# A two-layer mixture of experts around attention on one core: layer 0's first expert product gives its hidden values with inner channels in partitions, and both layers' gathers are issued one scatter earlier

## The reference, cut to what matters

```python
x = x + _L0_conv_ref(_gn(x), ...)          # layer 0: 1024 tokens of 192 channels
t = _to_tokens(x)
t = t + _L1_attn_ref(_ln_t(t), ...)        # 12 heads of 16
t = t + _L1_ffn_ref(_ln_t(t), ...)         # layer 1

def _L0_conv_ref(x, gate_w, fc1_w, fc1_b, fc2_w, fc2_b, ...):
    xf = x.reshape(-1, C)
    scores = softmax(xf @ gate_w.T)
    top_v, top_i = top_k(scores, 2)        # weights normalised to sum 1
    for e in range(8):
        w_e = sum(where(top_i == e, top_v, 0.0))
        h = _gelu(xf @ fc1_w[e].T + fc1_b[e])     # 192 -> 512
        y = h @ fc2_w[e].T + fc2_b[e]             # 512 -> 192
        out = out + w_e[:, None] * y
    shared = _gelu(xf @ w1_w.T + w1_b) * (xf @ w3_w.T + w3_b) @ w2_w.T + w2_b
    return out + shared
# layer 1: 16 experts, silu(x @ wg_e) * (x @ wu_e) @ wd_e with 384 inner channels, top 2, and a shared expert
```

## Time and profile before

| what | value |
|---|---|
| runs (3) | 442.01, 443.23, 445.12 us; median 443.23 |
| the profiled execution | 443.67 us, of which the span from first to last instruction 441.6 us |
| PE busy | 405.3 us (92%), granted clock 0.996 of full on average |
| DVE busy | 261.9 us (59%) |
| ACT busy | 186.4 us (42%) |
| POOL busy | 128.2 us (29%) |
| chain that ended last | PE 81%, ACT 6%, DVE 5%, DMA 5%, issue 2% |
| layer 0's blocks | first product of block 0 at 55.82 us, second product of block 22 at 143.25 us |

### The profile page before, as it was taken

How to read it: one execution, slowest core, us unless ns; L and a number is a source line. 1 busy time by engine, 2 the same in 40 slices (tenths; PEclk the granted TensorE clock), 3 DMA queues, 4 the chain that set the end, 5 groups by cost and what they waited for, 6 DMA issues and landing times.

```text
span 441.6 us, 7990 instructions
## 1 busy us (share of the span) xinstructions
PE 405.3 (92%) x2303; PEld 299.3 (68%) x2304; DVE 261.9 (59%) x673; ACT 186.4 (42%) x463; POOL 128.2 (29%) x137
## 2 busy tenths in 40 slices
PE   0899998999999999988888877999899999999996
PEld 0755455776776998866666655745677888878885
DVE  3526424222222286789898974474587777777743
ACT  1124231222222125898787863331444445454410
POOL 4300224555554100000000000001265555555540
PEclk9999999999999999999999999899999999999999
DMA  8999301111100496000000086870011111110006
GB/s 207 279 272 356 73 22 37 39 46 46 42 24 10 143 299 265 1 1 1 1 1 1 2 230 199 204 212 14 16 36 37 43 35 39 45 50 23 0 0 214
DMA packets 17432, 39.41 MB, mean 89 GB/s; under 512 B 5711, under 2 KB 10869, under 8 KB 16962
## 3 DMA queue, kind: packets, MB, share of 16 engines
q1 hardware_dynamic: 9186, 29.66, 22.8%
q0 software_dynamic: 5280, 6.85, 5.3%
q10 hardware_dynamic: 2944, 2.62, 1.8%
HBM read 36.21 MB, written 7.93 MB: 100 GB/s over the span
## 4 chain that ended last, share of the span: by engine, by line
PE 81%; ACT 6%; DVE 5%; DMA 5%; issue 2%; ACTq 0%; DVEq 0%; SPq 0%; POOLq 0%
PE bank L1376 13%; PE bank L1287 12%; PE bank L1349 9%; PE bank L1354 9%; PE bank L1549 5%; PE bank L1365 5%; PE bank L1503 4%; PE bank L1565 3%; PE bank L1331 3%; DMA w_first<-y_rows 3%; PE bank L1360 2%; PE bank L1359 2%; PE bank L1273 2%; PE bank L1597 2%; ACT xn_t L760 2%
## 5 line engine op out<-in xcount | busy, mean ns | idle before, releaser
L554 POOL DMA_INDIRECT rows<-xn_rows,slot_tok x56 | 59.7, 1066 | 89.4 <-DVE slot_tok L940 53.2
L562 POOL DMA_INDIRECT y_rows<-y,slot_row x54 | 55.4, 1027 | 79.1 <-DVE y L1008 41.9
L1376 PE MATMUL bank<-w_second,hid_t 128*128 x370 | 69.4, 327 | 2.8 <-DVE hid_t L993 2.8
L1376 PEld LDWEIGHTS bank<-w_second,hid_t 128*128 128x128 f32 x370 | 58.8, 190 | 3.6 <-issue 3.5
L1354 PE MATMUL bank<-w_first,rows_t 128*128 x124 | 45.3, 488 | 0.4 <-issue 0.4
L1010 DVE TENSOR_TENSOR y<-bank,w_second 128x192 f32<-128x192 f32 x23 | 8.2, 357 | 60.3 <-PE bank L1376 60.3
L993 DVE COPY hid_t<-bank 128x384 f32<-128x384 f32 (+1 forms) x54 | 33.0, 612 | 18.0 <-PE bank L1365 12.9
L1349 PE MATMUL bank<-w_first,rows_t 96*128 (+1 forms) x92 | 43.4, 594 | 0.1
L659 ACT ACTIVATE act_h<-bank 128x512 f32<-128x512 f32 x23 | 13.7, 597 | 65.0 <-PE bank L1349 65.0
L602 POOL COPY act_h<-o_inv 128x256 f32<-128x256 f32 x12 | 4.8, 400 | 121.7 <-DVE o_inv L1174 121.7
L664 ACT ACTIVATE act_g<-bank 128x384 f32<-128x384 f32 x31 | 15.2, 491 | 49.0 <-PE bank L1360 49.0
(11 more groups left out here) (198 smaller groups left out, 791.1 us busy)
## 6 DMA issues: line engine op xcount, KB each, us to landing
w_first<-in_gate_up SPq DMA_DIRECT2D x16, 384.0 KB, 5.8
w_second<-in_down SPq DMA_DIRECT2D x1, 4608.0 KB, 17.4
w_first<-in_fc SPq DMA_DIRECT2D x1, 3072.0 KB
w_second<-in_fc SPq DMA_DIRECT2D x1, 3072.0 KB, 29.0
w_first<-in_gate_up_rest SPq DMA_DIRECT2D x16, 192.0 KB, 6.5
rows<-xn_rows,slot_tok POOLq DMA_INDIRECT x56, 2.7
y_rows<-y,slot_row POOLq DMA_INDIRECT x54, 2.3
w_first<-in_x_t SPq DMA_DIRECT2D x2, 384.0 KB, 4.6
```

What stands on the lines that cost most here:

```text
L554: pool.indirect_dma_start(rows[b % 2][:, 0:ROW[L.l]], None, xn_rows[L.l], bass.IndirectOffsetOnAxis(slot_tok[:, b:b + 1].bitcast(U32), 0), ...
L562: pool.indirect_dma_start(y_rows[L.l], bass.IndirectOffsetOnAxis(slot_row[:, b:b + 1].bitcast(U32), 0), y[b % 2][:], None, bounds_check=TO ...
L1376: ins = pe.matmul(bank[:, 1, 0:C], hid_t[:, tile(ic)], w(P, ic * C, C), start=(ic == 0), stop=(ic == L.IC - 1))
```

## The change

In layer 0 the first product is turned round: the expert's 128 x 128 pieces of weights are held and the rows stream past, which gives the hidden values with inner channels in partitions. It takes 8 matmuls of 128 columns for the 2 of 512. Gelu writes them straight into the tile that the second product holds (`act_h` and `hid_t` in turn, `hid_b`); the 4 hidden transposes and DVE's copy go. A held operand is read here from a fixed place, so DVE copies the block's weights (97 x 1024 values, 2 instructions) from `w_first` into one of two buffers `first_w` two blocks ahead (`copy_weights`). The copies for blocks 0 and 1 come in front of the last shared product on DVE. In both layers POOL issues the gather of b+4 in front of the scatter of b.

```diff
+        hid_b = [act_h, hid_t]
+        first_w = [scratch_at(2048 + u * NCH * I0, NCH, I0) for u in range(2)]
...
             for b in range(L.NB):
-                scatter(b)
                 if b + AHEAD <= L.NB:
                     pool.wait_ge(L.rows_t_ps, b + AHEAD - 1)
                     gather(b + AHEAD)
+                scatter(b)
...
+        def act_block0(act, L, b, u):
+            act.wait_ge(L.first_ps, b + 1)
+            nc.scalar.activation(hid_b[u][:], bank[:, 5, :], ACT.Gelu).then_inc(L.hid_ready, 1)
...
+            def copy_weights(L, b, u):
+                at = dve.value_load(blk_weights[0:1, 0, bass.ds(b, 1)], min_val=0, max_val=(L.E - 1) * L.sizes[0])
+                if not isinstance(b, int) or b >= 2:
+                    dve.wait_ge(L.first_ps, b - 1)
+                for k in range(NCH):
+                    w = w_first[0:CH + k, k * I0:(L.E - 1) * L.sizes[0] + (k + 1) * I0][:, bass.ds(at, I0)]
+                    v.tensor_copy(first_w[u][0:CH + k, k, :], w).then_inc(L.first_w_ready, 1)
             def blocks(L):
                 dve.wait_ge(s_fc2b, 16)
-                dve.wait_ge(L.expert_ready, len(L.sizes))
-                hid_copy(L, 0)
+                copy_weights(L, 2, 0)
                 result(L, 0, 0, 0)
-                hid_copy(L, 1)
+                copy_weights(L, 3, 1)
                 result(L, 1, 1, 0)
                 w_low_parts()
-                with dve.Fori(0, (L.NB - 3) // 2) as i:
+                with dve.Fori(0, (L.NB - 5) // 2) as i:
                     for u in range(2):
-                        b = i * 2 + (u + 3)
-                        hid_copy(L, b - 1)
-                        result(L, b - 1, u, i + 1)
+                        b = i * 2 + (u + 4)
+                        copy_weights(L, b, u)
+                        result(L, b - 2, u, i + 1)
...
+                elif s == "first weights":
+                    dve.wait_ge(s_fc1, 32)
+                    dve.wait_ge(L.expert_ready, len(L.sizes))
+                    copy_weights(L, 0, 0)
+                    copy_weights(L, 1, 1)
...
                 pe.wait_ge(L.rows_t_ready, b + 1)
                 if L.l == 0:
-                    for k in range(NCH):
-                        kr = CH + k
-                        ins = pe.matmul(bank[:, 5, :], rows_t[0:kr, k, :], w(kr, k * I0, I0),
-                                        start=(k == 0), stop=(k == NCH - 1))
+                    pe.wait_ge(L.first_w_ready, NCH * (b + 1))
+                    if not isinstance(b, int) or b > 0:
+                        pe.wait_ge(L.hid_ready, b)
+                    for ic in range(L.IC):
+                        for k in range(NCH):
+                            kr = CH + k
+                            ins = pe.matmul(bank[:, 5, tile(ic)], first_w[u][0:kr, k, tile(ic)], rows_t[0:kr, k, :],
+                                            start=(k == 0), stop=(k == NCH - 1))
...
-            def second(L, b, w, first_block=False):
-                pe.wait_ge(L.hid_t_ready, b + 1)
+            def second(L, b, w, u, first_block=False):
+                hid = hid_t if L.l else hid_b[u]
+                pe.wait_ge(L.hid_t_ready if L.l else L.hid_ready, b + 1)
...
+            def blocks_first(L, down):
+                first(L, 0, None, 0)
+                rows_transpose(L, 1, 1, 0)
+                first(L, 1, None, 1)
+                rows_transpose(L, 2, 0, 1)
+                second(L, 0, down, 0, True)
+                down = weights(L, 1, 1)
+                first(L, 2, None, 0)
+                rows_transpose(L, 3, 1, 1)
+                second(L, 1, down, 1)
+                with pe.Fori(0, (L.NB - 3) // 2) as i:
+                    down = weights(L, i * 2 + 2, 1)
+                    for u in range(2):
+                        b = i * 2 + (u + 3)
+                        first(L, b, None, 1 - u)
+                        rows_transpose(L, b + 1, u, i + 2)
+                        second(L, b - 1, down, u)
+                        if u == 0:
+                            down = weights(L, b, 1)
+                second(L, L.NB - 1, weights(L, L.NB - 1, 1), (L.NB - 1) % 2)
```

More of the change, by code:

```diff
@@ L443, in build @@
                 ["best0", "best1", "top2", 0, "pads", 1, "ended", "expert", "blocks", "places", 2, "slots", 3, "weights", 4, "diag0", 5,
-                 "diag1", 6, 7]),
+                 "diag1", 6, "first weights", 7]),
             1: ([(0, 1), (1, 0), "count", (1, 1), "rank", (2, 0), (2, 1), "expert", (3, 0), "slots", (3, 1), (4, 0),
@@ L654, in act_rows @@
                            ).then_inc(L.rows_t_ready, 1)
+        def act_block0(act, L, b, u):
+            act.wait_ge(L.first_ps, b + 1)
+            nc.scalar.activation(hid_b[u][:], bank[:, 5, :], ACT.Gelu).then_inc(L.hid_ready, 1)
         def act_block(act, L, b):
             act.wait_ge(L.first_ps, b + 1)
-            if L.l == 0:
-                nc.scalar.activation(act_h[:], bank[:, 5, :], ACT.Gelu).then_inc(L.hid_ready, 1)
-            else:
-                if not isinstance(b, int) or b > 0:
-                    act.wait_ge(L.hid_ready, b)
-                nc.scalar.activation(act_g[:], bank[:, 5, 0:I1], ACT.Silu).then_inc(L.gate_act, 1)
+            if not isinstance(b, int) or b > 0:
+                act.wait_ge(L.hid_ready, b)
+            nc.scalar.activation(act_g[:], bank[:, 5, 0:I1], ACT.Silu).then_inc(L.gate_act, 1)
         def rest_of(start):
@@ L699, in act_blocks @@
         def act_blocks(act, L):
-            act_block(act, L, 0)
+            act_block0(act, L, 0, 0)
             act_rows(act, L, 1)
@@ L1396, in blocks @@
                 rows_transpose(L, 2, 0, 1)
-                second(L, 0, weights(L, 0, 1), True)
+                second(L, 0, weights(L, 0, 1), 0, True)
                 hid_transpose(L, 1)
@@ L1400, in blocks @@
                 rows_transpose(L, 3, 1, 1)
-                second(L, 1, weights(L, 1, 1))
+                second(L, 1, weights(L, 1, 1), 1)
                 with pe.Fori(0, (L.NB - 3) // 2) as i:
@@ L1411, in blocks @@
                         rows_transpose(L, b + 1, u, i + 2)
-                        second(L, b - 1, w2)
+                        second(L, b - 1, w2, u)
                         if u == 0:
@@ L1415, in blocks @@
                 hid_transpose(L, L.NB - 1)
-                second(L, L.NB - 1, weights(L, L.NB - 1, 1))
+                second(L, L.NB - 1, weights(L, L.NB - 1, 1), (L.NB - 1) % 2)
             pe.wait_ge(s_const, 16)
@@ L1462, in _ @@
                     pe.wait_ge(L0.expert_ready, len(L0.sizes))
-                    w0 = weights(L0, 0, 0)
-            blocks(L0, w0)
+                    down = weights(L0, 0, 1)
+            blocks_first(L0, down)
             def norm_transposes(which, half):
```

24 lines of the change are left out of this document (12 added, 12 removed).

## The result

| | before | changed |
|---|---|---|
| median, us | 442.22 (440.86 to 445.12, 6 runs) | 431.78 (429.67 to 432.66, 6 runs) |
| ratio | 1 | 0.9747, 95% interval 0.9719 to 0.9775 |
| profiled execution, us | 443.67 | 431.16 |
| its span, us | 441.6 | 429.1 |

The forecast was 433.0 in a range of 430 to 438.5. The runs of one program also differ by the clock that TensorE is granted (the kernel before took 440.9 to 443.0 us where its mean was 1.00, 443.8 to 445.8 at 0.996 and 447.3 to 447.8 at 0.989), so where a median is moved by that I compare stretches of the traces.

The account below looks back on a forecast made before the run. PE's stream was taken to bound layer 0's steady blocks. Gains of 2.2 (start), 7.4 (steady blocks) and 0.6 us (end) sum to 10.2; 443.67 less these, less 0.44 to the median, gives 433.0 us, range 430 to 438.5.

Parts of the forecast that it names:

- Hidden transposes: Layer 0's steady blocks: four transposes per block go, taking 0.44 us off PE's stream in each.
- The turned product: Layer 0's first product: 16 passes of 128 columns, 0.11 us each with loads hidden, take 1.75 us for 1.72.
- Steady period: Layer 0's steady blocks: period falls from 3.71 to 3.30 us, 7.4 us gained over 18 periods.
- The waits in front of the first product: Layer 0, PE before each first product: rows' copy ends 0.5 us before it is due; costed at nothing.
- first rival: Layer 0, before the first product: PE needs about 0.85 us to go on, waits eat the gain, 439 us; chance 0.10.
- VectorE's copies: Layer 0, two weight copies per block on DVE at 0.60 us each, 0.7 spare; nothing in the steady state.
- First blocks: Start of layer 0: block 4 starts at 69.6 instead of 71.77 us, still behind `w_low`; 2.2 us gained.
- Last block: End of layer 0: first to second product 4.14 instead of 4.70 us, waiting for block 21's y; 0.6 gained.
- The gathers: POOL's order, both layers: gather ahead of scatter keeps rows in time; taken as 0, between -0.5 and +0.5 us.
- Third rival: Layer 0: DVE's weight copies and POOL's DMAs exclude each other, period 4.2 us, total 449 us; chance 0.05.

Follow-up runs that it names:

- the changed kernel's second trace: The changed kernel unaltered, run again beside the version with mended ends: 432.93 us, ratio 0.9783; layer 0 took 79.23 us instead of 77.19.
- the transposes put back: Changed kernel plus four transposes of a constant into an unused bank before each second product of layer 0: 442.67 us, ratio 1.0002.
- the triple ones: Changed kernel with each weight copy made three times in blocks 4 to 21, the extra ones into free places: 438.6 us, ratio 0.991.
- Versions with more room: The changed kernel repeated (432.93 us) and with layer 0's ends mended (432.44); rows' copy ahead of gelu on the mended kernel (433.32) and the changed one (431.42).

## Why the prediction was right, step by step

It was right in its mechanism for layer 0: PE's stream bounds the steady blocks, and what is taken off it is gained as long as the rows come in time. How close the numbers came is partly luck. The sum for layer 0 was 10.2 us and measured 10.24, but its parts missed by -0.3, +0.5 and -0.15 (points 3, 6 and 7), and the changed kernel's second trace would have given 8.2. The median came out 1.2 us under the forecast, and 1.0 of that is the kernel before, whose median over six runs is 442.22 and not the 443.23 over three from which the forecast was taken; against 442.22 the medians differ by 10.4. Layer 1's 1.1 us, which the forecast lacks, don't show in that. The clock may hide them: three of the changed kernel's six runs had a mean of 0.996, and those of the six before are not on record. The two traces, one with a dip of the clock before and one without after, differ by 12.5.

1. **Hidden transposes**, 0.44 a block: right, and shown to be PE's stream by the transposes put back.
2. **The turned product**, 16 passes at 0.11: right. They start 0.110 and 0.113 us apart in turn, 1.79 together for the 1.75 forecast. The Trainium skill's rule ("TensorE: Matmul & The Clock Gate", section "The mechanism") that loads overlap matmuls in flight only where their row groups differ is contradicted again: these 16 loads share their rows.
3. **Steady period** 3.30: measured 59.67 / 18 = 3.315; 7.1 us gained for 7.4.
4. **The waits in front of the first product**: rightly costed at nothing, with less room than the text allowed. Of the 0.5 us 0.24 are PE's own, which leaves 0.24. The first rival was near: its point of decision, 0.85 us for PE to go on, was not reached, but a ScalarE that is more than 0.24 late makes PE wait, which cost 1.6 and 2.1 us in two traces.
5. **VectorE's copies**: taken at 0.60 each, measured 0.34 from start to start and 0.76 for the pair. This is the double rate for float32 within SBUF that the Trainium skill gives ("VectorE: DVE Perf Modes", perf-mode tiers); the trace agrees with its 0.34 for 512 columns. The room in front of the first product was 0.92 and 1.17 us in turn instead of 0.7; the copies were shorter, but the steps in front of them took up to 0.97 instead of 0.6.
6. **First blocks**: block 4 at 13.27 after block 0, forecast 13.8; 2.7 gained for 2.2, by the shorter copies.
7. **Last block**: 4.25 for 4.14, with y of block 21 as the wait, as named.
8. **The gathers**: "with the old order and a period of 3.3 it would come late" was right and had no price. It is 8.6 us. The 0 that the step gives for the order, compared with the kernel before, holds only because turning and order come together; a reader who adds the steps would take the order for an ornament. For layer 1 the step was wrong: it saw 0.2 us to gain and expected periods kept to 0.02 us, and the order brought 1.1 (1.0 when changed alone), more than the 0.5 that it allowed. The gather's wait was the wrong row to price it by; the blocks that lost time in the kernel before are those in which PE's table load is long or starts late, as above, and by what the order keeps it from that is open.

Third rival: POOL gave way and VectorE did not, as its last sentences argued; they read it from an instruction with two SBUF inputs, and here it is copies. The Trainium skill's "SBUF — State Buffer", "SBUF: two separate sides", has the first comer hold the pair for its whole instruction. As far as POOL's spans tell, the trace disagrees: a copy that starts 0.15 us into a scatter (100.20 and 100.04 above) is not delayed, and scatters are stretched also by copies that start after them, where these go on long enough (1.70 beside the triple ones).

## What to carry to other kernels

Where one engine's stream sets the period, taking work off it pays in full only down to the next latency in the loop: list every transfer that must arrive once per period, add up its chain (here result, scatter, gather, 2.7 us to land) and compare it with the new period before believing the saving. Do the same with margins, and count the waiting engine's own restart; a margin of a quarter of a microsecond was used up in two of eleven traces. And test a change of two halves as a table of four: in layer 0 each half alone was worth 0.4 and 1.7 us of 10.2.

## What the runs showed of the hardware that I had not expected

**Table loads beside POOL.** In ten of the traces (all but the four of "Versions with more room"), a table load of ScalarE that starts 1.3 to 1.6 us after the start of an indirect DMA on POOL (0.3 to 0.6 after its usual end) took 0.39 us on average (224 loads, at most 0.48), one that starts 1.6 to 1.8 after it 0.28 (24 loads). PE's took up to 0.50 there, or as long after the end of a scatter that was stretched, and 0.30 elsewhere. VectorE's were not touched: 73 of them start 1.3 to 1.6 us after an indirect DMA, and none took over 0.35. A few loads far from any such DMA were long as well (ScalarE's first of layer 1, 0.49). It doesn't need a second DMA: in the changed kernel none follows, and ScalarE's loads there are as long, off the path. What POOL or its queue does at that moment stays open.

**A loop that takes longer with other code in front of it.** With four blocks of layer 0 written out, VectorE's loop of layer 1, whose code is the same, starts its table load 0.41 us after the branch instead of 0.31 in its steady turns (0.47 instead of 0.33 in the first). PE's transposes wait for what follows: one period in two is 3.65 instead of 3.55. Both kernels with the written-out blocks show it (108.93 and 108.94), none of the others does, nor do the two kernels whose VectorE code grew by double and triple copies. Where code lies in memory is a possible reason and wasn't tested.

**The clock.** In the profile before, TensorE's granted clock was below full in one stretch of attention, while expert weights were loading; after it was not (stretch and its length, then busy us of PE, PEld, DVE, ACT, POOL, granted clock, DMA share, GB/s). The kernel before, in two stretches:

```profile
275.00:280.00 5.00, 4.99 (x35) 4.66 (x35) 2.27 (x11) 1.27 (x3) 0.00 (x0) 1.00 0.36 105
280.00:285.00 5.00, 4.75 (x19) 2.90 (x19) 2.62 (x18) 2.44 (x3) 0.00 (x0) 0.69 1.03 254
```

and the changed one, in the second of them:

```profile
280.00:285.00 5.00, 5.00 (x21) 2.53 (x19) 3.22 (x11) 2.79 (x4) 0.00 (x0) 1.00 0.96 281
```

It fell from 2.4 to 1.2 GHz for 3.4 us from 281.9 on, with PE busy for the 5 before; that expert weights were loading is what the DMA share shows, not a cause. The stretch between the layers' blocks took 169.71 us with this and 168.37 without. The other traces say the same whatever they change: 167.9 to 168.4 at a mean clock of 0.999 or 1.000 (six kernels), 169.6 to 169.8 at 0.996 (five), 173.3 at 0.988 (one). So 1.3 us of the two profiles' difference are not the change's.
